# Expert scatter of a token model's last layer: indirect transfers released by the shared expert's products instead of by their own completions

## What is computed

```
h2      = rmsnorm(X, norm2_w).reshape(T, 256)            # T = 2048 tokens
logits  = h2 @ router_w                                  # 8 experts
topw, topi = top_k(softmax(logits), 2);  topw = softmax(topw)
shared  = (silu(h2 @ sh_gate) * (h2 @ sh_up)) @ sh_down  # every token, width 512
eout[e] = (silu(h2 @ e_gate[e]) * (h2 @ e_up[e])) @ e_down[e]
out     = X + shared + sum over the two chosen experts of topw * eout
```

## Time and profile before

| what | value |
|---|---|
| time of the kernel, median of 3 runs (lowest to highest) | 908.37 us (907.36 to 908.58) |
| time of the profiled execution | 907.34 us |
| span from its first to its last instruction | 905.4 us |
| what lies around the span | 1.9 us |
| mean granted TensorE clock | 0.953 of full |
| busy: PE, DVE, ACT, POOL | 799.7, 463.1, 333.5, 148.6 us |
| start of the shared expert, of the slots | 546.6 us, 661.2 us |

### The profile page before, as it was taken

How to read it: one execution, slowest core, us unless ns; L and a number is a source line. 1 busy time by engine, 2 the same in 40 slices (tenths; PEclk the granted TensorE clock), 3 DMA queues, 4 the chain that set the end, 5 groups by cost and what they waited for, 6 DMA issues and landing times. The chain is left out here.

```text
span 905.4 us, 18245 instructions
## 1 busy us (share of the span) xinstructions
PE 799.7 (88%) x6868; PEld 533.5 (59%) x6869; DVE 463.1 (51%) x1079; ACT 333.5 (37%) x568; POOL 148.6 (16%) x155
## 2 busy tenths in 40 slices
PE   4798999999879987999998879875989999999994
PEld 2366666666568874666666754542646666666662
DVE  7766666665546544667664774600133444433441
ACT  4666666666524443555552222100011111111110
POOL 5000000000013431000000220273002222222222
PEclk9999999999969997999998888986999999999997
DMA  5200000000012672899964400023012222332321
GB/s 191 106 1 2 2 3 2 2 2 2 3 42 70 139 152 59 140 171 198 163 120 140 135 0 14 34 104 109 24 47 42 46 46 42 47 47 47 47 41 19
DMA packets 68489, 58.81 MB, mean 65 GB/s; under 512 B 5504, under 2 KB 60104, under 8 KB 68432
## 3 DMA queue, kind: packets, MB, share of 16 engines
q1 hardware_dynamic: 60512, 47.60, 23.3%
q0 software_dynamic: 7152, 9.38, 6.5%
q10 hardware_dynamic: 768, 1.02, 0.4%
HBM read 35.02 MB, written 22.95 MB: 64 GB/s over the span
## 5 line engine op out<-in xcount | busy, mean ns | idle before, releaser
L1128 DVE TENSOR_REDUCE fa_m<-ps 128x2 bf16<-128x512 f32 x128 | 81.8, 685 | 35.1 <-PE ps L1026 34.4
L1375 POOL DMA_INDIRECT out<-ex_Y,ex_to x39 | 60.6, 1553 | 216.0 <-DVE ex_Y L1625 212.9
L1108 ACT ACTIVATE fa_PT<-ps 128x1024 f32<-128x1024 f32 x64 | 65.5, 1024 | 68.3 <-PE ps L1044 68.3
L628 ACT ACTIVATE la_PT<-ps 128x512 f32<-128x512 f32 x128 | 69.5, 595 | 37.0 <-PE ps L532 37.0
L1443 PE MATMUL ps<-WG,ex_xT 128*128 x156 | 74.3, 599 | 0.6 <-ACT ex_xT L1503 0.6
L1456 PE MATMUL ps<-WD,ex_hT 128*128 x312 | 73.9, 380 | 0.9 <-DVE ex_hT L1609 0.9
L1443 PE MATMUL ps<-WU,ex_xT 128*128 x156 | 74.2, 598 | 0.0
L1505 ACT ACTIVATE ex_sl<-ps 128x512 f32<-128x512 f32 x39 | 23.3, 597 | 135.1 <-PE ps L1443 135.1
L1605 DVE TENSOR_TENSOR ex_hd<-ps,ex_sl 128x512 f32<-128x512 f32 x39 | 27.0, 692 | 80.1 <-PE ps L1443 80.1
L661 DVE TENSOR_REDUCE la_m<-ps 128x4 bf16<-128x512 bf16 x64 | 44.1, 688 | 43.7 <-PE ps L525 43.7
L642 DVE CAST V<-ps 96x512 bf16<-96x512 f32 x64 | 44.0, 687 | 34.5 <-PE ps L497 34.5
(11 more groups left out here) (255 smaller groups left out, 1399.2 us busy)
## 6 DMA issues: line engine op xcount, KB each, us to landing
QK<-qk_parts SPq DMA_DIRECT2D x96, 128.0 KB, 4.8
qk_parts<-pj_parts SPq DMA_DIRECT2D x16, 384.0 KB, 2.7
expert_in<-zfill SPq DMA_DIRECT2D x1, 5070.0 KB, 16.2
ex_XR<-expert_in SPq DMA_DIRECT2D x39, 130.0 KB
WG<-in_e_gate SPq DMA_DIRECT2D x8, 512.0 KB, 8.9
WU<-in_e_up SPq DMA_DIRECT2D x8, 512.0 KB, 9.4
WD<-in_e_down SPq DMA_DIRECT2D x8, 512.0 KB, 8.4
out<-HS SPq DMA_DIRECT2D x4, 512.0 KB, 3.1
```

What stands on the lines that cost most here:

```text
L628: nc.scalar.activation(PT[:, n // 2 % 2, jh, n % 2], ps[:, 2 * (n % 2) + jh], ACT.Exp, scale=QK_SCALE).then_inc(s_exp[jh], 1)
L1108: nc.scalar.activation(PT[:, grp % 2, k:k + 2], ps[:, 2 + 2 * (hp % 2):4 + 2 * (hp % 2)].rearrange("p k (j i) -> p k j i", j=2), ACT.Exp, ...
L1128: nc.vector.reduce_max(m[:, par, h], ps[:, h % 2].rearrange("p (f j) -> p f j", f=2), AX.X).then_inc(s_max, 1)
L1375: nc.gpsimd.indirect_dma_start(out=outs, out_offset=bass.IndirectOffsetOnAxis(ap=to[:, n:n + 1], axis=0), in_=Y[:, n], in_offset=None, com ...
```

## The change

The ring of four semaphores becomes one, `s_sc`, which each of the 32 transfers raises by 16. A transfer no longer waits for an earlier one. Instead every third one (k = 0, 3, ..., 30) waits until DVE has made product number min(6 + k / 3, 16), counted from one: the sixth product releases k = 0 to 2, the seventh k = 3 to 5, and so on, the sixteenth k = 30 and 31. The wait for `s_pos` ahead of all of them stays. SP waits for the one semaphore to reach 32 x 16 = 512 instead of for four to reach 128.

```
-    RING = 4
-    s_sc = [sem("ex_scattered" + n) for n in names(RING)]
+    s_sc = sem("ex_scattered")
...
-                for r in range(RING):
-                    sp.wait_ge(s_sc[r], NT * 2 // RING * 16)
+                sp.wait_ge(s_sc, NT * 2 * 16)
...
-                        if k >= RING:
-                            pool.wait_ge(s_sc[k % RING], k // RING * 16)
+                        if k % 3 == 0:
+                            pool.wait_ge(s_act_, min(FC + 2 + k // 3, 4 * FC))
                         nc.gpsimd.indirect_dma_start(out=g.xs, out_offset=bass.IndirectOffsetOnAxis(ap=pidx[:, n, t:t + 1], axis=0),
-                                                     in_=g.XS[:, t], in_offset=None).then_inc(s_sc[k % RING], 16)
+                                                     in_=g.XS[:, t], in_offset=None).then_inc(s_sc, 16)
```

## The result

| | before | changed |
|---|---|---|
| median (lowest to highest), 4 runs each | 907.87 us (907.33 to 908.58) | 883.17 us (881.17 to 886.21) |
| ratio, with its 95% interval | | 0.973 (0.9695 to 0.9766) |
| profiled execution, its span | 907.34, 905.4 us | 886.21, 884.1 us |

The change makes the kernel 24.7 us faster on the chip on which the two were compared. That addition matters: on three other chips the kernel before takes 879 to 888 us itself, as the experiments show. Every one of these times is of an execution whose instructions were recorded; what the recording does to them stays open (see the end of the part on the prediction).

A forecast was written before the change was run, and what follows sets the result against it. PE's signals, held back by an unbroken train of scatters, were taken to bound the shared expert. Span 905.4 - 23.4 + 1 = 883.0, plus 1.9 for the profiled execution and 1.0 for the median: 886.0 us forecast, range 883 to 888.5.

The forecast's parts named there:

- the likeliest case: Whole kernel: signals on time once the train of scatters is cut, 886.0 us, 22.4 faster, range 883 to 888.5, chance 0.60.
- What bounds the kernel: Middle of the shared expert: an unbroken train of scatters holds PE's signals back, 35.8 us of the chain unexplained.
- The size: Shared expert: with PE's stalls and half clock gone, down(3) starts at 628.5 instead of 651.89, 23.4 us earlier.
- Lateness left over: down(1)'s signal to acc(1): may feel the end of the first train, costing 1 us, bounds 0 and 2.1.
- The signs: Trace after: three trains, two rests of 4 to 6 us, down(3) at 628 to 630, XR turn 637.8 to 639, slots 244 us.
- Rival 1: Second and third trains: lateness returns within a train, about 895 us for one (chance 0.12), 903 for two (0.07).
- XR: Start of the slots: XR is loaded by 637.5, 0.3 us before PE needs it; cost 0 to 1 us, taken as 0.
- The output writes: Behind the XR loads on SP: four writes nearly together take 6.5 us, hidden before the first addition; cost 0.
- The rule on ports: Skill's rule: engine and DMA ports are disjoint, so scatters could not hold PE back and the gain would be 0.
- Rival 2: Shared expert: the scatters are not the cause, lateness stays, 908.4 us; chance 0.09 with all that ends near zero.
- Rival 3: Products 8 to 15: every product carries a late signal, 930 us, or 914 in a milder form; chance 0.12.
- Rival 4: POOL's waits: products are long made when asked for, so the train stays whole; no separate chance given.

The follow-up runs named there:

- the kernel with ten scatters in the first train: The changed kernel, but the sixth product releases four scatters and the sixteenth only one, so trains of 10, 12 and 10; 885.34 us beside 907.09, chip 4.
- ring and paced: The kernel before, its ring of four semaphores kept, with the changed kernel's waits on products added; 884.28 us on chip 6, ratio 1.0007 to the kernel before.
- the late train: The changed kernel with one wait alone, all 32 scatters unbroken once product 8 is made; 908.62 us beside 907.17 on chip 13.
- a ring of two: The kernel before with two semaphores instead of four, so each scatter waits until the second before it has landed; 884.23 us on chip 6, ratio 0.9998.
- the paced kernels: Kernels whose scatters wait on products: the changed kernel, 883.17 us; four scatters released first, 885.34; three output writes issued before the XR load, 880.82 and 884.30.

## Why the prediction was right, point by point

**The time.** 886.0 was forecast and 883.2 measured, within the likeliest case's own 883 to 888.5. On the profiled execution the sum was 884.9, and it took 886.2. The step from there to the median was wrong: the median was put 1.0 above the profiled execution and lies 3.0 below it, since the four runs spread over 5 us, from 881.17 to 886.21, where those of the kernel before spread over 1.3. That the median still lies in the range is no merit of that term. And it is luck that the two kernels were compared on a chip with lateness.

**What bounds the kernel.** Right for the chip of the trace: the unexplained 35.8 us were late signals of PE, and with them gone PE runs through. Incomplete as a statement on the kernel: on chips 6, 2 and 8 no trace, with an unbroken train or without, has such a piece. One trace could not tell this. What in it spoke was the name, "another core or an unknown queue", for a wait that the program can't explain, and on chip 4 even that name is missing.

**The size.** From the start of the first pair to down(3) the kernel before took 651.89 - 546.56 = 105.3 us and the changed one 629.61 - 547.45 = 82.2: 23.2 gained, 23.4 forecast. The remaining terms of the profiled execution: it reached the shared expert 0.9 us later (not touched by the change: in the fourteen traces here that moment lies between 541.2 and 548.3), the first turn came 0.6 later after down(3), and from the turn to the end it took 244.6 instead of 244.2. Together 905.4 - 23.2 + 0.9 + 0.6 + 0.4 = 884.1.

**Lateness left over.** Forecast 1 us (0 to 2.1), measured 0: acc(1) started 0.04 behind down(1). The case that I feared shows in the kernel with ten scatters in the first train, 1.1 late.

**The signs.** The three trains, the start of down(3) and the length of the slots came as forecast. The first rest, 3.9 us, lies just below the 4 to 6, and the first turn of `XR`, at 639.53, 0.5 us behind the 637.8 to 639, by the 0.9 and the 0.6 us above.

**The onset**, put between 9 and 16 us into a train, is now narrower: on time at 11.6 us in (pair 12 of the changed kernel, second train), 1.1 us late at 13.2 (ten scatters first, half a microsecond after their end). Within a train that still runs, the earliest late one is due 16.1 us in. Rival 1 was thus nearer than I thought, as the train of 12 runs to 15 us; it decided nothing, since no signal of PE falls in its last 3 us.

**XR.** Right: its load went out 5.7 us after down(3) began, 5.8 forecast, and it was not waited for.

**The output writes** are the term that was mis-sized: "hidden, 0", measured 0.6, though not where I looked for it. I named the first addition as their customer and worked out that it can wait. The one that couldn't was PE's read of the expert's number, a small load in nobody's list of transfers, which takes twice as long while three writes are under way.

**The rule on ports.** On chips 6, 2 and 8 nothing contradicts it: 32 scatters in a train, and no compute engine slower by anything that the traces show. On chips 4 and 13 signals of PE are held back by a train of scatters, with the matmuls themselves at their usual pace (1.88 us for four), so it is not the ports, of which the Trainium skill (SBUF — State Buffer, "Who interferes with whom") speaks, that would have to give way. A gain of 0 is what chip 6 shows (ring and paced, 1.0007), and chips 2 and 8, where no paced kernel ran, have no lateness to take away; but that comes from the missing lateness and says nothing for the rule.

**The other rivals.** Rival 2, "the scatters are not the cause", falls by the late train, whose lateness moved with it. Rival 3 needed lateness within the first 4 us of a train; none was seen before 11.6. Rival 4 falls by the three trains.

**What stays open.** Why chips 4, 13 and 15 and the first one do this and 6, 2 and 8 don't, and whether it is the chip or its condition: all runs on one of chips 2 to 15 were made together. Whether age or the number of scatters in a train counts. Whether the bytes or the number of transfers count. Whether small rests (a ring of two) are enough. And whether the lateness exists when nothing is recorded: every time in this document is of an execution whose instructions were recorded (each has its own span and granted clock), and the missing rises make the recording itself a suspect. If it is the cause, the change may gain nothing where nothing is recorded.

## What to carry to other kernels

A wait on the critical path that no instruction of the trace explains, or a signal that comes long after the work behind it ended, is worth more attention than its share, and worth a second trace on another chip before a change is credited with removing it: the gain of pacing here is 20 to 26 us or nothing, by the chip. Where a long row of small indirect transfers has slack, it can be given out a few at a time against the work that it runs beside: on chip 6, without the lateness, that cost nothing that the times show, and on four chips with it the paced kernels took 20 to 26 us less than the kernel before. Whether the gain is there without recording has to be timed first. When transfers are moved, look for small reads of registers beside their new place, and issue what is ready ahead of what must wait.

## What the runs showed of the hardware

- The kernel before takes 884.3 us (median of 25, 881.1 to 887.9) on chip 6, 879.0 and 882.8 on chip 2 and 884.0 on chip 8, and 907.1 to 907.9 on chips 4, 13 and the first one and 904.3 (901.5 to 907.8) on chip 15. On the first chip, 4 and 13, signals of PE come up to 24 us late in an unbroken train of 32 indirect scatters; on 6, 2 and 8 none does. Signals of ACT and DVE are not seen late in it: product 9 on chip 4 starts 0.03 us after its Silu.
- A signal of PE due 11.6 us into a train was on time, and one due 13.2 us after the start of ten scatters, 0.5 us after their end, 1.1 us late. In trains of 32, those due 16 to 21 us in were 6.6 to 23.8 us late, and the last late one came 4.6 to 4.8 us after the last scatter's issue had ended.
- A scatter of 128 rows is issued in 0.96 us and every 1.27 us, whether its rows have 260 floats or 16.
- The first read of one number by PE's sequencer takes 0.49 us with no large write under way and 1.09 to 1.12 with three output writes of 512 KB under way.
